# Cross-attention with 20 heads on one core: the row maxima's stores and loads go from SyncE's queue to ScalarE's

## The reference

```python
q = _split_heads(hidden_states @ w_q, HEADS)          # x: (16, 256, 320), 20 heads of 16
k = _split_heads(text @ w_k, HEADS)                   # text: 248 of the 256 context rows (16, 256, 512)
v = _split_heads(text @ w_v, HEADS)
out_text = _merge_heads(_sdpa(q, k, v))
k_ip = _split_heads(ip_h @ w_k_ip, HEADS)             # ip_h: 4 dummy and 4 image rows
v_ip = _split_heads(ip_h @ w_v_ip, HEADS)
out_ip = _merge_heads(_sdpa(q, k_ip, v_ip, mask=mask_ip))
out = (out_text + IP_SCALE * out_ip) @ w_out + b_out + residual
```

## Time and profile before

| | us |
|---|---|
| median of 3 runs | 558.0 (553.15 to 563.45) |
| the profiled execution | 556.4 |
| its span, first to last instruction | 554.6 |
| second stage: first key scores of batch 0 to the start of the last exponential | 211.75 to 541.93 |

### The profile page before, as it was taken

One profiled execution on the slowest core, in us unless ns is written; L12 is line 12 of the kernel. 1 busy time (PEld: TensorE's weight loads), 2 busy tenths in 40 slices (PEclk: granted clock), 3 DMA queues, 4 the chain that ended last, 5 costly groups with the idle time before them and its releaser, 6 DMA issues.

```text
span 554.6 us, 12517 instructions
## 1 busy us (share of the span) xinstructions
PE 481.5 (87%) x4304; PEld 323.7 (58%) x4304; DVE 384.9 (69%) x706; ACT 280.3 (51%) x355; POOL 127.9 (23%) x205
## 2 busy tenths in 40 slices
PE   3979899999999586799799889897987988989985
PEld 2868687887887463455455555554554555555542
DVE  2739425325325256899779989897997999999932
ACT  3633335344344013666556666565664666666671
POOL 6014000000000000432323332331332433332341
PEclk9989999999999787999979999999998999999999
DMA  8978888888788935672681762672754654763211
GB/s 271 362 266 149 259 298 273 309 268 293 272 261 270 345 120 179 200 243 74 204 261 33 247 221 89 234 233 79 235 170 154 219 154 144 245 204 103 72 52 47
DMA packets 94195, 112.49 MB, mean 203 GB/s; under 512 B 14304, under 2 KB 72992, under 8 KB 94144
## 3 DMA queue, kind: packets, MB, share of 16 engines
q1 hardware_dynamic: 93296, 109.89, 60.6%
q0 software_dynamic: 848, 1.90, 1.9%
HBM read 73.17 MB, written 38.63 MB: 202 GB/s over the span
## 4 chain that ended last, share of the span: by engine, by line
PE 48%; DMA 15%; issue 11%; SPq 10%; DVE 9%; ACT 4%; POOL 3%; DVEq 0%; ACTq 0%; POOLq 0%
PE pv L730 10%; DMA max_rows<-row_buf 10%; PE score_t L716 5%; PE pj L739 4%; PE score_q L666 3%; ACT probs L471 3%; SPq L278 3%; PE score_t L625 3%; PE score_t L626 3%; PE score_t L627 3%; SPq L285 2%; PE pj L625 2%; DMA q_stack<-max_rows 2%; PE pj L627 2%; PE pj L626 2%
## 5 line engine op out<-in xcount | busy, mean ns | idle before, releaser
L534 DVE TENSOR_REDUCE max_cols<-score_q 128x4 fp32r<-128x992 f32 x160 | 187.1, 1170 | 46.4 <-PE score_q L666 41.1
L471 ACT ACTIVATE probs<-score_t 128x1024 f32<-128x1024 f32 x160 | 163.4, 1021 | 72.0 <-PE score_t L716 71.9
L730 PE MATMUL pv<-probs,v_cur 128*32 128x256 f32 x1920 | 124.5, 394 | 0.6 <-ACT probs L471 0.6
L387 POOL TENSOR_TENSOR o_turned<-o_turned,inv_cols 128x256 f32<-128x256 f32 x80 | 49.8, 622 | 179.7 <-DVE inv_cols L589 179.7
L716 PE MATMUL score_t<-q_stack,k_stack 64*128 64x256 f32 x440 | 56.5, 335 | 29.4 <-ACT probs L471 17.6
L730 PEld LDWEIGHTS pv<-probs,v_cur 128*32 128x32 f32 x1920 | 55.3, 111 | 41.1 <-issue 4.6
L462 ACT ACTIVATE o_all<-pv 128x512 f32<-128x512 f32 x80 | 47.8, 598 | 60.7 <-PE pv L730 60.7
L716 PEld LDWEIGHTS score_t<-q_stack,k_stack 64*128 64x128 f32 x440 | 33.8, 189 | 74.8 <-ACT probs L471 37.7
L739 PE MATMUL pj<-wo_sb,o_all 128*128 128x320 f32 x192 | 69.0, 468 | 2.9 <-DVE o_all L594 2.2
L381 POOL TENSOR_TENSOR x_all<-x_all,bias_sb 128x640 f32<-128x640 f32 x16 | 24.9, 1554 | 192.5 <-DMA x_all<-in_x 192.5
L586 DVE STREAM_TRANSPOSE o_turned<-o_all 128x512 f32<-128x512 f32 x80 | 56.1, 702 | 11.9 <-ACT o_all L462 11.9
(11 more groups left out here) (134 smaller groups left out, 719.5 us busy)
## 6 DMA issues: line engine op xcount, KB each, us to landing
q_stack<-q_parts SPq DMA_DIRECT2D x33, 320.0 KB, 4.5
k_stack<-k_parts SPq DMA_DIRECT2D x33, 320.0 KB, 5.6
v_rows<-v_out SPq DMA_DIRECT2D x32, 320.0 KB, 2.4
v_cur<-v_rows SPq DMA_DIRECT2D x16, 640.0 KB
o_all<-in_ctxT SPq DMA_DIRECT2D x16, 512.0 KB, 5.2
q_parts<-qk_out SPq DMA_DIRECT2D x32, 256.0 KB, 2.5
k_parts<-qk_out SPq DMA_DIRECT2D x32, 248.0 KB, 4.7
x_all<-in_x SPq DMA_DIRECT2D x16, 320.0 KB, 3.3
```

The lines of the kernel that those rows point to most:

```text
L387: pool.tensor_tensor(out, out, inv_cols[:, k, :].unsqueeze(2).broadcast_to([P, 2 * S // 32, DH]), ALU.mult).then_inc(scaled, 1)
L471: nc.scalar.activation(probs[:, slot(u, p), :], score_t[:, :], ACT.Exp, scale=SCALE)\
L534: nc.vector.tensor_reduce(out=max_cols[:, h, :, at:at + 4:2].rearrange("p t e -> p e t"), in_=both[:, :, :, 0:TEXT], op=ALU.max, axis=AX.X ...
L730: last = mm(pv[32 * t:32 * t + 32, at:at + S], values_of(u, kind, 4 * k + t), probs[:, slot(u, 2 * k + t // 2), a:a + S], start=kind != 1, ...
```

## The change

The two functions move to ACT and their calls are placed in its order of pairs. ACT issues the load of rows (b, 1) ahead of pair 2's exponential, the store of rows (b + 1, 0) ahead of pair 6's, the load of rows (b + 1, 0) ahead of pair 8's, and the store of rows (b, 1) behind pair 0's exponential and copy. For batch 0 it issues store, load, store, load in a row ahead of the first exponential. SP's list loses these calls and keeps its order otherwise. No computation changes.

```diff
 @block.sync
-            def store_rows(b, h):
-                sp.wait_ge(rows_turned, 2 * b + h + 1)
-                sp.dma_start(max_rows[h].rearrange("r (t i n) -> i r t n", t=2, i=4),
-                             row_buf[:, h, :].rearrange("p (t n) -> p t n", t=2)).then_inc(rows_stored, 16)
-            def load_rows(t, h):
-                sp.wait_ge(rows_stored, 16 * (2 * t.b + h + 1))
-                dst = q_stacks[t.w][2 * DH - 1::2 * DH, h * HALF * S:(h + 1) * HALF * S]
-                sp.dma_start(dst.rearrange("p (a n) -> p a n", a=HALF).bitcast(f32),
-                             max_rows[h][0:4 * HALF, :].rearrange("(a x) n -> x a n", x=4)).then_inc(rows_loaded[h], 16)
             def group(g):
...
                 for j in range(3, 6):
                     store_qk(g, j)
-                    if not more and j == 3:
-                        store_rows(0, 0)
-                        load_rows(Turn(0, 0), 0)
...
-            store_rows(0, 1)
-            load_rows(Turn(0, 0), 1)
             sp.wait_ge(tile_ready, 10 * GROUPS)
             load_kaux(2)
...
             def batch(t):
-                ahead, next_, first = t.there(2), t.there(1), isinstance(b, int) and b == 0
-                if not first:
-                    load_rows(t, 1)
+                ahead, next_ = t.there(2), t.there(1)
...
                     load_values(b + 1, 1 - u)
-                    store_rows(b + 1, 0)
-                    load_rows(t.to(1), 0)
-                    store_rows(b + 1, 1)
 @block.scalar
+            def store_rows(b, h):
+                act.wait_ge(rows_turned, 2 * b + h + 1)
+                act.dma_start(max_rows[h].rearrange("r (t i n) -> i r t n", t=2, i=4),
...
+            def load_rows(t, h):
+                act.wait_ge(rows_stored, 16 * (2 * t.b + h + 1))
...
+                act.dma_start(dst.rearrange("p (a n) -> p a n", a=HALF).bitcast(f32),
...
             def batch(t):
                 b, u = t.b, t.u
+                next_, first = t.there(1) and t.there(), isinstance(b, int) and b == 0
                 for p in range(PAIRS):
+                    if p == 2 and t.there() and not first:
+                        load_rows(t, 1)
+                    if p == 6 and next_:
+                        store_rows(b + 1, 0)
+                    if p == 8 and next_:
+                        load_rows(t.to(1), 0)
                     if t.there():
                         act.wait_ge(st_ready, PAIRS * b + p + 1)
...
                     for k, off in EVACUATE.get(p, ()):
                         if t.there(off):
                             evacuate(b + off, (u + off) % 2, k)
+                    if p == 0 and t.there() and not first:
+                        store_rows(b, 1)
+            for h in range(2):
+                store_rows(0, h)
+                load_rows(Turn(0, 0), h)
             batches(act, batch)
```

More of the change, by code:

```diff
@@ L457, in _ @@
             groups(act, group)
+            def store_rows(b, h):
+                act.wait_ge(rows_turned, 2 * b + h + 1)
+                act.dma_start(max_rows[h].rearrange("r (t i n) -> i r t n", t=2, i=4),
+                             row_buf[:, h, :].rearrange("p (t n) -> p t n", t=2)).then_inc(rows_stored, 16)
+            def load_rows(t, h):
+                act.wait_ge(rows_stored, 16 * (2 * t.b + h + 1))
+                dst = q_stacks[t.w][2 * DH - 1::2 * DH, h * HALF * S:(h + 1) * HALF * S]
+                act.dma_start(dst.rearrange("p (a n) -> p a n", a=HALF).bitcast(f32),
+                             max_rows[h][0:4 * HALF, :].rearrange("(a x) n -> x a n", x=4)).then_inc(rows_loaded[h], 16)
             def evacuate(b, u, k):
```

## The result

The changed kernel takes 578.0 us, median of four (574.5 to 589.7), beside 558.2 for the kernel before on the same chip. The ratio is 1.037, with a 95% interval of 1.023 to 1.050: slower by over 2%, as forecast. The profiled execution has a span of 573.1 us, 18.5 more than before.

The account below looks back on a forecast made before the run. PE, busy 87%, was taken to bound the kernel, with eight row-load waits of 13.2 us. Profiled: 556.4 - 10.6 - 2.0 + 22 + 3.0 = 568.8 us; forecast 570.4 by the median, own range 561 to 581, overall 552 to 598.

Parts of the forecast that it names:

- The second half, 22 us: ACT's wait for the store's landing delays pair 2's exponential 2.0 us; 1.47 reach PE in each of batches 1 to 15.
- SP no longer waits for this store, so its next DMAs move up: SP's output store, residual and stack start as ACT's second-half row store is under way; its landing taken as 3.2 us.
- The first half, nothing, at most 0.6 us a batch: ACT's store ahead of pair 6 and load ahead of pair 8 fit its idle time; upper bound if landing takes 5.25 us.
- a landing of up to 3.9 us: First half's store, issued at 310.0, has 3.9 us until pair 7's exponential ends, more than the 2.99 us landing.
- the rival in which the backlog follows the store: SP's transfers slow ACT's store to 5.25 us; second half 57, first half 9; 616 us; chance 0.15, full or part.
- What comes back, 10.6 us and half of the clock: PE's row waits return 10.6 of 13.2 us; clock lost in batches 3 and 10 returns 2.0 of 4.1 us.
- The start, 3.0 us: Ahead of batch 0, ACT's store, load, store, load delay its first exponential 4.7 us; 3.0 estimated, between 0 and 4.7.
- The dear issue: Rival: an issue on ACT takes twice 0.57 us, adding 0.57 a batch ahead of pair 2; 579 us, chance 0.08.
- the two rules weighed: DMA engines alternate between queues, favouring the 22 us or less; issuers share the same 16 engines, pointing to 57 us.

Follow-up runs that it names:

- SP's hold: Changed kernel, with SP waiting in batches 0, 1 and 15 until ACT's second-half row store has landed: 566.4 us, ratio 1.016 to the kernel before.
- the idle run: Kernel before, with four further DMAs a batch on ACT at the change's places, moving data nobody uses, row transfers still on SP: 571.0 us, ratio 1.024.

## Why the prediction was right, and where its sizes were off

*The forecast and its mechanism held.* ACT waits for landings, this costs more than PE's waits had, and the time is inside the forecast's own range. The run with the loads behind the exponentials shows that ACT's waits ahead of pairs 2 and 8 are most of the loss of the steady batches (10.1 of some 14.6 us), and SP's hold shows that batch 1 and batch 15 are the same kind of wait, behind traffic that SP sent before the store. That the total lies in the range is luck in part. The terms added up to 12.4 us and the profiled executions differ by 18.5: the first half cost 7.3 us more than I put and the start 4.6 more, the clock gave 2.1 more back, the second half cost 1.3 less, and the projections ran 1.9 us quicker. Together that is the difference to half a microsecond.

*The second half, 22 us.* The sum is close and its distribution wrong. I put 1.47 us on each of fifteen batches. In the thirteen middle ones it is 0.56, 7.3 us in all. In batch 4 pair 2's exponential comes 1.0 us late, not 2.0: ACT starts the store 0.08 us after the copy, at the low end of my bounds, and it lands in 2.35 us, under the 2.67 that I took for the lowest (the trace before has such landings too, 234.07 to 236.39 in batch 1, outside the rows I had read). Batch 1 lost 9.1, part of it clock, and batch 15 with the end 4.3. That these make up the 22 us again, at 20.7, is luck. The step that failed is "SP no longer waits for this store, so its next DMAs move up", which I priced once for all batches with 0.2 us of landing. In most batches the output store waits for DVE and keeps SP behind the row store. In batch 1 there is no output to store, so nothing held SP, and in batch 15 the output store went first.

*The first half, nothing, at most 0.6 us a batch.* It is 0.56 on the mean and up to 1.4, 7.3 us in the middle batches. This step failed: I had taken a landing of up to 3.9 us as given. It is 5.7 to 6.9 us for the rows of batches 3 to 14, where SP's queue had 4.5 to 6.5. Here the rival in which the backlog follows the store was right, and its 9 us for this half were near. For the second half it came true in batches 1 and 15 alone.

*What comes back, 10.6 us and half of the clock.* The row waits went, and the clock in the middle batches came back whole, 4.1 us instead of 2.0. The clock's loss moved to batches 0 (0.76, 0.84 before), 1 (0.88, 1.00 before) and 15 with the end (0.95, 0.99 before).

*The start, 3.0 us.* Batch 0 took 3.0 us more and started 2.9 later against the projections, with 1.7 us of batch 1's former row wait (2.04, of which 0.32 stay) saved inside it, so some 7.6 us in this term, over the 4.7 of its high end. I had looked at ACT's first exponential alone. It came at 217.63, near the 216.9 that I gave, by luck: the store was issued 1.9 us earlier and took 2.7 longer to land. What I overlooked is the first half: its store waits in ACT's order for the last copy, and PE's first key scores wait for its load (2.76 us). Putting the start back on SP is worth 5.65 us in the two profiled executions (3.08 in the start and 2.57 in batch 0) and 5.9 by the medians (555.25 to 549.33). By the ratios it is about half of that, and their intervals overlap, so the whole time alone doesn't show it.

*The dear issue* falls: 0.53 us an issue, and the loads and stores of the idle run cost 0.2 us a batch. All of that lies at the store behind pair 0's copy. In the changed kernel this store holds up pair 1's exponential by 0.24 us, where I had put 0.4. The delay lies within the wait at pair 2 and is left when the wait goes.

Of the two rules weighed, no run showed the turns between queues shortening a landing behind SP's loads: 5.85 us on ACT's queue in batch 4, 5.25 on SP's, 8.78 in batch 1. The other, that issuers share the same engines, fits all of them (the Trainium skill, "DMA: Bandwidth & Descriptors", sections "Queues, rings and completion order" and "Issuing engines are not separate DMA queues"). Why the turns don't help this store was not settled. One thing the traces show: the row store lands about as long after the first of SP's stack loads whichever queue it is on. Before, in batch 4, the loads start at

```profile
304.52 2.20 SPq L278 DMA_DIRECT2D q_stack<-q_parts  x3
```

and the row lands at 316.87, 12.35 us later. After, it lands 12.68 us behind them in batch 4 and 12.27 in batch 1, where the store was issued 6.8 and 3.5 us after the first load. Over batches 0 to 13 before it is 12.3 to 14.3 us, and over batches 1 to 13 after 12.3 to 13.3. In the three runs with the first half alone on ACT, where some stores go out ahead of SP's load of the values, the spread is wider, 9.6 to 14.0. So it seems to be the loads in flight that set the landing, more than the queue or the moment of issue; no run tested this by itself.

## What to carry to other kernels

A DMA that is moved to a compute engine brings its wait with it, and everything behind it in that engine's order pays. Put the dependent load behind the last instruction that doesn't need it and ahead of the next that waits for something else; one instruction later was worth 16 us here (578.0 to 561.6), and places behind the next copy or pair lost 24 (549.3 to 573.7). Before giving a small transfer a queue of its own, look at what is issued before it on the other queues, and in the first and last batches above all, where a wait that kept the order elsewhere may be missing.

## What the runs showed of the hardware

A queue of its own did not let a 32 KB store pass SP's loads: it landed 5.7 to 6.9 us after issue behind them, once 8.78, and in 2.35 us ahead of them. ACT starts a DMA while an activation that stands ahead of it is still running (311.00, with the copy from 310.92 to about 311.52), but the next activation starts only when the issue has ended: pair 1's exponential came at 311.65, 0.73 us after the copy's start instead of 0.49. A hundred further kilobytes a batch that nobody waited for made the kernel before 13 us slower, with PE's waits for SP's row loads up by 6.4 us and the mean clock down from 0.972 to 0.952.
